# One double-width product for F and an earlier B0 in a two-layer adapter kernel (one Trainium2 core)

## The chip, the cores and the metric

The kernel runs on one core of one Trainium2 chip. The metric is the device time of one execution in microseconds. The core has TensorE (PE in the profile, its weight loads PEld), VectorE (DVE), ScalarE (ACT), GpSimd (POOL) and SyncE (SP); each of them works through its instructions in the order in which they are written, and they wait for one another on semaphores. All transfers are issued from the SP queue.

## The reference

Two linear layers with low-rank adapters, each added to its input, on x of 8 x 256 rows and 1024 columns in float32. Cut to what matters:

```python
# layer 0: 4 x 512 rows; one of 5 adapters per group, rank 32
x = x + x @ W0.T + 0.5 * (x @ A0[label]) @ B0.T
# layer 1: 8 x 256 rows; one of 32 adapters per row group, rank 16
x = x + x @ W1.T + b + 2.0 * (x @ A1[slot]) @ B1[slot]
```

The labels pick the adapters at run time.

## The kernel before

The two layers are folded into one matrix. With D = I + W0 and E = I + W1, the product E D is made first on the chip (the first stage), and then applied to x in two further stages of two 512-row chunks each. Each of the three products is done by a seven-product scheme over 512 x 512 blocks (`ORDER`: A11 B11, A12 B21, S1 T1, ...), in which S1 to S4 and T1 to T4 are sums of blocks made on VectorE.

Each float32 operand is split into a rounded part (h, made on ScalarE, line 233) and the remaining part (l, made on VectorE, line 234), and each product of blocks is done in three passes: h h, h l, l h. A block product has four output tiles of 128 x 512 and four quarters of the inner dimension, so 48 products of 128x128 weights and 512 columns.

Beside the block products stand small ones for the adapters. In the first stage these are: D, the rows B0 times the blocks of W1 (`down`, lines 472 to 479), C, the blocks of W0 times A1 (`across`, lines 481 to 488), and F, B0 times A1 (lines 540 to 543). For F the stationary operand is a 128-column tile of `b0s`, in which the rounded part of B0 stands in columns 0 to 31 and 64 to 127, and the remaining part in columns 32 to 63; the moving operand is A1's rounded part (`a1s[0]`) or remaining part (`a1s[1]`), 128 columns each, 8 quarters of the inner dimension each: 16 products into one bank of PSUM. The rows of the result that belong to the rounded and the remaining part of B0 are then added (`rows_sum`, lines 494 to 497: a copy on ScalarE, an add on VectorE) and put into four row groups (`four_rows`, lines 499 to 504). `fsrc` is used only in the second stage (`load_a0`, `low_f`).

The order of TensorE's work is the order in which `pe(...)` is called. After A11 B11 come `down` (eight products), `across` (twelve), F (sixteen), and then tile 0 of A12 B21. The order on ScalarE, VectorE, GpSimd and SP isn't written out: `Plan.rehearse` goes through all jobs with an assumed duration for each and gives each job a due time, from TensorE's rehearsed time backwards; a lane takes, of the jobs whose inputs are there soonest, the one that is due first. A job whose `due` is set by hand in the code keeps it if it is the earlier one. Loading A1 needs the labels: SP reads eight labels from `label_t` into registers (line 194) and issues eight transfers, one for each slot (line 451).

Of the kernel before, what the change touches and what calls it, by code (L numbers as in the profile page):

```python
# [6 lines left out]
ALU = mybir.AluOpType  # L7
F32 = mybir.dt.float32
F32R = mybir.dt.float32r
# [10 lines left out]
NK = 8  # L20
# [101 lines left out]
def bass_blocks(nc, x, labels, w0, a0, b0, w1, bias, a1, b1, out):  # L122
    ctx = ExitStack()
    with ctx:
        def sb(name, shape, dt, where=None):
            return (where or ctx).enter_context(nc.sbuf_tensor(name, shape, dt))
# [9 lines left out]
        bstk = [sb(f"bstk{n}", [128, 1024], F32R) for n in range(2)]  # L136
        mb = {n: sb("m_" + n, [128, 4, 512], F32) for n in ("11", "12", "21", "22")}
        small = ExitStack()
        a1s = [sb(f"a1{j}", [128, NK, 128], F32R, small) for j in "hl"]
        a1raw = sb("a1raw", [128, 8, NK, 16], F32, small)  # L140
        b0s = sb("b0s", [128, NK, 4, R], F32R, small)
        ct = [sb(f"ct{j}", [128, 512], F32R, small) for j in "hl"]
# [12 lines left out]
        dtmp = [sb(f"dtmp{n}", [R, 512], F32, temps) for n in range(3)]  # L155
# [8 lines left out]
        ps = [ctx.enter_context(nc.psum_tensor(f"ps{i}", [128, 512], F32)) for i in range(8)]  # L164
# [7 lines left out]
        plan = Plan()  # L172

        def tk(*name):
            return tokens.setdefault(name, Token())
# [4 lines left out]
        def act(waits, emit, token, took):  # L180
            plan.put("act", waits, emit, token, took)

        def dve(waits, emit, token, took):
            plan.put("dve", waits, emit, token, took)
# [4 lines left out]
        def transfer(waits, pairs, s, token, kb, numbers=(), top=0, count=1):  # L189

            def emit(eng):
                for i in numbers:
                    if i not in label:
                        label[i] = eng.value_load(label_t[:, i:i + 1], min_val=0, max_val=top)  # L194
                for dst, src in pairs():
                    eng.dma_start(dst, src).then_inc(s, 16)  # L196
            plan.put("sp", list(waits) + ([tk("labels")] if numbers else []), emit, token, 0.45 * count)
            plan.jobs[-1].kb = kb
            counts[s] = counts.get(s, 0) + 16 * count
            token.sem, token.value = s, counts[s]  # L200

        bank_free = {}

        def pe(out_ap, lhs, rhs, start, waits=(), name=None):
            n = 1
            for s in rhs.shape[1:]:
                n *= s
            plan.put("pe", waits, (out_ap, lhs, rhs, start), tk(*name) if name else Token(), max(n / 2400 + 0.0133, 0.107))
            plan.jobs[-1].named = bool(name)
# [11 lines left out]
        act([tk("eye")], lambda e: e.activation(eye_r[:, :], eye[:, :], ACT.Copy), tk("eye_r"), 0.3)  # L221
        dve([], lambda e: e.memset(astk[:, :, :, 64:128].bitcast(F32), 0.0), tk("zero"), 0.9)
        transfer([], lambda: [(label_t[:, :], labels)], s_lab, tk("labels"), 1)
        plan.jobs[-1].due = 7.0
        transfer([], lambda: [(bias_t[:, :], bias)], s_bias, tk("bias"), 4)


# [27 lines left out]
        def split_b(n, ks):  # L255

            stage, name = n // 7, ORDER[n % 7][1]
            src = where[stage, name][:, ks[0]:ks[-1] + 1, :]
            used = [4 * n + k - NB for k in ks]
            spare = [tk("Bk", m // 4, m % 4) for m in used if m >= 0]  # L260
            hi, lo = (br[j][:, slot(n, ks[0]):slot(n, ks[-1]) + 1, :] for j in range(2))
            split([tk("f", stage, name, k) for k in ks], spare, src, hi, lo, same(("B", 0, n), ks), same(("B", 1, n), ks), len(ks))
# [31 lines left out]
        def ybank(stage, i):  # L294
            return 4 - 4 * (stage % 2) + i
# [145 lines left out]
        for k in range(4):  # L441
# [2 lines left out]
            split_a(0, (k,))  # L444
            split_b(0, (k,))
        transfer([], lambda: [(b0raw[:, :, :].rearrange("p k r -> p (k r)"), b0[:, :])], s_b0, tk("b0"), 128)
        act([tk("b0")], lambda e: e.activation(  # L447
            b0s[:, :, :, :], b0raw[:, :, :].unsqueeze(2).to_broadcast([128, NK, 4, R]), ACT.Copy), tk("b0h"), 1.1)
        dve([tk("b0h")], lambda e: e.tensor_tensor(  # L449
# [44 lines left out]
        def rows_sum(bank, done, cols, dst, name, spare):  # L494

            act([done] + spare, lambda e: e.activation(dtmp[0][:, cols], ps[bank][R:2 * R, cols], ACT.Copy), tk("t", *name), 0.6)
            dve([tk("t", *name)], lambda e: e.tensor_tensor(dst, ps[bank][0:R, cols], dtmp[0][:, cols], ALU.add), tk("sum", *name), 0.7)

        def four_rows(src, dst, ready, name):

            for q in (0, 1, 3):
                act([ready], lambda e, q=q: e.activation(dst[q * R:(q + 1) * R, :], src, ACT.Copy, scale=S0), tk("four", q, *name), 0.65)
            dve([tk("four", 0, *name)], lambda e: e.scalar_tensor_tensor(
                out=dst[2 * R:3 * R, :], in0=src, scalar=S0, in1=dst[0:R, :].bitcast(F32), op0=ALU.mult, op1=ALU.subtract), tk("four", 2, *name), 0.7)
# [22 lines left out]
        Y = [ybank(0, i) for i in range(4)]  # L527
# [10 lines left out]
        for k in range(4):  # L538
            split_b(1, (k,))
        for k in range(NK):  # L540
            for j in range(2):
                pe(ps[Y[1]][:, 0:128], b0s[:, k, :, :].rearrange("p q r -> p (q r)"), a1s[j][:, k, :], k == 0 and j == 0,
                   [tk("b0l"), tk("a1", j, k // 4)], ("fd",) if (k, j) == (NK - 1, 1) else None)
        rows_sum(Y[3], tk("dn", 0), slice(0, 512), dtmp[1][:, :], ("e",), [])
        rows_sum(Y[1], tk("fd"), slice(0, 128), dtmp[2][:, 0:128], ("f",), [tk("sum", "e")])
        bank_free[Y[1]] = [tk("sum", "f")]
        four_rows(dtmp[2][:, 0:128], fsrc, tk("sum", "f"), ("f",))
        sum_s1(0)
        sum_t1(0)
# [405 lines left out]
```

How the kernel before makes its waits and increments, by code:

```python
def wait_all(eng, waits, done):  # L115
    for t in waits:
        if done.get(t.sem, 0) < t.value:
            done[t.sem] = t.value
            eng.wait_ge(t.sem, t.value)
# [71 lines left out]
            def emit(eng):  # L191
                for i in numbers:
                    if i not in label:
                        label[i] = eng.value_load(label_t[:, i:i + 1], min_val=0, max_val=top)
                for dst, src in pairs():
                    eng.dma_start(dst, src).then_inc(s, 16)
# [680 lines left out]
        def run(eng, name, s):  # L877
            done = {}
            for job in order[name]:
                wait_all(eng, job.waits, done)
                job.emit(eng).then_inc(s, 1)
# [3 lines left out]
            @block.sync  # L885
            def _(eng):
                done = {}
                for job in order["sp"]:
                    wait_all(eng, job.waits, done)
                    job.emit(eng)
                for s in s_keep.values():
                    eng.wait_ge(s, counts[s])
# [13 lines left out]
            @block.tensor  # L906
            def _(eng):
                done = {}
                wait_all(eng, [tk("fzero")], done)
                zeros = fstk[:, 0, :]
                for i in range(WARM):
                    ins = eng.matmul(ps[7][:, :], zeros, zeros.unsqueeze(1).to_broadcast([128, 4, 128]), start=True, stop=True)
                ins.then_inc(s_pe, 1)
                for job in tensor:
                    wait_all(eng, job.waits, done)
                    out_ap, lhs, rhs, first = job.emit
```

## Time and profile before

| what | value |
|---|---|
| time, median of 3 runs | 295.98 us (293.93, 295.98, 296.96) |
| profiled execution | 294.4 us, its span 292.7 us |
| TensorE (PE) busy | 286.7 us, 98% of the span |
| weight loads (PEld) busy | 239.6 us, 82% |
| VectorE busy | 223.2 us, 76% |
| ScalarE busy | 143.5 us, 49% |
| granted TensorE clock | 1.000 (mean of the core) |

The span runs from the first to the last instruction of one profiled execution, and times in the rows are counted from its start. A row of a timeline has the start, the duration, the engine, the line of the kernel, the operation and its output and inputs, how many like it were merged (x2), and in brackets the idle time of the engine before it and what ended that. Matmuls overlap, so the distance from start to start tells their pace, not the duration. Buffer numbers are left out of names, so `ar0h` is the rounded left operand of products 0, 2, 4 and `ar1h` that of 1, 3, 5.

### The profile page before, as it was taken

What the parts mean: (1) busy time and instruction counts of PE and PEld (TensorE: products, weight loads), DVE (VectorE), ACT (ScalarE), POOL (GpSimd) and SP (SyncE); (2) the same over time, 40 slices, a digit from 0 to 9 for tenths busy, and PEclk for the clock granted to TensorE, in tenths of its full rate; (3) what the DMA queues carried; (4) which work ended last, traced back from release to release, by engine and by line L of the source; (5) the groups of instructions that cost most, each with busy time, mean ns of one, the idle gap of its engine ahead of it and who ended that gap; (6) DMA issues with size and microseconds to landing.
All of it is one profiled execution on the core that took longest, in us unless ns stands there. A gap on an engine that the chain in (4) does not pass through costs nothing.

```text
span 292.7 us, 3668 instructions
## 1 busy us (share of the span) xinstructions
PE 286.7 (98%) x1340; PEld 239.6 (82%) x1340; DVE 223.2 (76%) x265; ACT 143.5 (49%) x194; POOL 5.0 (2%) x13
## 2 busy tenths in 40 slices
PE   8979999999999999999999999999999999999996
PEld 5858888888888888888888888888988888888885
DVE  5557998898988989999985999839295956687400
ACT  5377539452563862827282632637474463505021
POOL 0000300000000000010000000000010000000000
PEclk9999999999999999999999999999999999999999
DMA  7389800220645101116432438240101100012222
GB/s 252 93 301 394 271 2 2 72 73 0 202 114 152 36 2 36 36 24 172 168 113 68 140 106 290 91 129 37 38 0 72 72 2 0 0 72 91 91 99 81
DMA packets 18628, 29.21 MB, mean 100 GB/s; under 512 B 2994, under 2 KB 5426, under 8 KB 18610
## 3 DMA queue, kind: packets, MB, share of 16 engines
q1 hardware_dynamic: 18610, 28.98, 30.2%
q8 instruction: 10, 0.16, 0.2%
q14 instruction: 8, 0.07, 0.1%
HBM read 20.58 MB, written 8.39 MB: 99 GB/s over the span
## 4 chain that ended last, share of the span: by engine, by line
PE 93%; SPq 3%; DMA 2%; issue 1%; ACT 0%; DVE 0%
PE ps L917 93%; SPq L196 2%; SPq L194 1%; DMA label_t<-in_labels 1%; DMA b0raw<-in_b 1%; ACT b0s L447 0%; DVE b0s L449 0%; DVE keep_s L731 0%
## 5 line engine op out<-in xcount | busy, mean ns | idle before, releaser
L917 PE MATMUL ps<-brh,ar0h 128*128 128x512 f32 (+1 forms) x180 | 69.2, 390 | 0.1
L917 PE MATMUL ps<-brl,ar0h 128*128 128x512 f32 (+1 forms) x180 | 68.3, 385 | 0.0
L917 PE MATMUL ps<-brh,ar0l 128*128 128x512 f32 (+1 forms) x180 | 68.2, 384 | 0.0
L233 ACT ACTIVATE brh<-w_B 128x1024 fp32r<-128x1024 f32 (+1 forms) x40 | 38.8, 969 | 57.6 <-PE ps L917 50.6
L917 PE MATMUL ps<-brh,ar1h 128*128 128x512 f32 x160 | 62.5, 391 | 0.0
L917 PE MATMUL ps<-brl,ar1h 128*128 128x512 f32 x160 | 62.3, 390 | 0.0
L917 PE MATMUL ps<-brh,ar1l 128*128 128x512 f32 x160 | 62.3, 389 | 0.0
L234 DVE TENSOR_TENSOR brl<-w_B,brh 128x1024 fp32r<-128x1024 f32 (+1 forms) x40 | 44.5, 1113 | 18.5 <-ACT brh L233 18.3
L917 PEld LDWEIGHTS ps<-brh,ar0h 128*128 128x128 f32 x180 | 34.3, 191 | 7.4 <-ACT ar0h L233 0.8
L917 PEld LDWEIGHTS ps<-brh,ar0l 128*128 128x128 f32 x180 | 33.8, 188 | 6.8
L917 PEld LDWEIGHTS ps<-brl,ar0h 128*128 128x128 f32 x180 | 33.9, 188 | 6.5
L917 PEld LDWEIGHTS ps<-brh,ar1l 128*128 128x128 f32 x160 | 30.0, 188 | 6.4
L917 PEld LDWEIGHTS ps<-brh,ar1h 128*128 128x128 f32 x160 | 30.1, 188 | 6.0
L917 PEld LDWEIGHTS ps<-brl,ar1h 128*128 128x128 f32 x160 | 30.1, 188 | 5.9
L234 DVE TENSOR_TENSOR ar0l<-w_A,ar0h 128x1024 fp32r<-128x1024 f32 (+1 forms) x16 | 17.3, 1086 | 0.8 <-ACT ar0h L233 0.5
L344 DVE SCALAR_TENSOR_TENSOR keep_s<-ps,bias_t,keep_s 128x512 f32<-128x512 f32 x16 | 11.6, 747 | 6.7 <-PE ps L917 6.6
L233 ACT ACTIVATE ar0h<-w_A 128x1024 fp32r<-128x1024 f32 (+1 forms) x16 | 15.0, 945 | 1.6 <-DVE w_A L281 0.8
L234 DVE TENSOR_TENSOR ar1l<-w_A,ar1h 128x1024 fp32r<-128x1024 f32 (+1 forms) x14 | 14.9, 1068 | 0.7 <-ACT ar1h L233 0.5
L386 ACT ACTIVATE keep_s<-ps,bias_t 128x512 f32<-128x512 f32 x7 | 4.8, 687 | 21.3 <-PE ps L917 21.3
L281 DVE TENSOR_TENSOR w_B<-w_B 128x1024 f32<-128x1024 f32 x12 | 14.4, 1220 | 0.2
L233 ACT ACTIVATE ar1h<-w_A 128x1024 fp32r<-128x1024 f32 (+1 forms) x14 | 12.9, 929 | 0.6 <-PE ps L917 0.5
L917 PE MATMUL ps<-pstk,dstk 128*128 128x512 f32 x32 | 12.4, 389 | 0.0
(116 smaller groups left out, 355.7 us busy)
## 6 DMA issues: line engine op xcount, KB each, us to landing
w_B<-in_x SPq DMA_DIRECT2D x32, 256.0 KB, 2.8
out_z<-keep_s SPq DMA_DIRECT2D x23, 256.0 KB, 2.0
w_B<-in_w SPq DMA_DIRECT2D x16, 256.0 KB, 5.1
w_A<-in_w SPq DMA_DIRECT2D x16, 256.0 KB, 4.9
raw<-in_b SPq DMA_DIRECT2D x64, 32.0 KB, 1.7
out_z<-keep_w SPq DMA_DIRECT2D x8, 256.0 KB, 2.1
raw<-in_a SPq DMA_DIRECT2D x8, 128.0 KB, 2.2
a1raw<-in_a SPq DMA_DIRECT2D x8, 64.0 KB, 1.8
```

The lines of the kernel that those rows point to most:

```text
L194: label[i] = eng.value_load(label_t[:, i:i + 1], min_val=0, max_val=top)
L196: eng.dma_start(dst, src).then_inc(s, 16)
L233: act(waits + spare, lambda e: e.activation(hi, src, ACT.Copy, scale=scale), h, 0.2 + 0.43 * wide)
L234: dve([h], lambda e: e.tensor_tensor(lo, src, hi.bitcast(F32), ALU.subtract), l, 0.15 + 0.54 * wide)
L281: lambda e, part=part, ins=ins: e.tensor_tensor(place[:, part, :], ins[0], ins[1], op),
L344: dve(waits + [tk("bias")], lambda e: e.scalar_tensor_tensor(out=dst, in0=z, scalar=bias_t[:, 4 * a + i:4 * a + i + 1], in1=other, op0=ALU ...
L386: act([done, tk("bias"), tk("stored", stage, "s1", i, 0, 0)], lambda e: e.activation(s1, z, ACT.Identity, bias=bias_t[:, 4 + i:5 + i]), to ...
L917: ins = eng.matmul(out_ap, lhs, rhs, start=first, stop=False, skip_group_check=True)
```

## The change

`a1s` becomes two halves of one tile `a1hl` in which, for each quarter of the inner dimension, the 128 columns of the rounded part and the 128 of the remaining part lie side by side. F is computed by one product of 256 columns for each quarter, eight in all; `rows_sum` works on 256 columns, and one more VectorE add puts the two halves of 128 columns together. The transfer of the labels gets a due time of 4.0 in place of 7.0, and that of B0 a due time of 9.0, which it didn't have.

```diff
-        a1s = [sb(f"a1{j}", [128, NK, 128], F32R, small) for j in "hl"]
+        a1hl = sb("a1hl", [128, NK, 2, 128], F32R, small)
+        a1s = [a1hl[:, :, j, :] for j in range(2)]
...
         transfer([], lambda: [(label_t[:, :], labels)], s_lab, tk("labels"), 1)
-        plan.jobs[-1].due = 7.0
+        plan.jobs[-1].due = 4.0
...
         transfer([], lambda: [(b0raw[:, :, :].rearrange("p k r -> p (k r)"), b0[:, :])], s_b0, tk("b0"), 128)
+        plan.jobs[-1].due = 9.0
...
         for k in range(NK):
-            for j in range(2):
-                pe(ps[Y[1]][:, 0:128], b0s[:, k, :, :].rearrange("p q r -> p (q r)"), a1s[j][:, k, :], k == 0 and j == 0,
-                   [tk("b0l"), tk("a1", j, k // 4)], ("fd",) if (k, j) == (NK - 1, 1) else None)
+            pe(ps[Y[1]][:, 0:256], b0s[:, k, :, :].rearrange("p q r -> p (q r)"), a1hl[:, k, :, :].rearrange("p j c -> p (j c)"), k == 0,
+               [tk("b0l"), tk("a1", 0, k // 4), tk("a1", 1, k // 4)], ("fd",) if k == NK - 1 else None)
         rows_sum(Y[3], tk("dn", 0), slice(0, 512), dtmp[1][:, :], ("e",), [])
-        rows_sum(Y[1], tk("fd"), slice(0, 128), dtmp[2][:, 0:128], ("f",), [tk("sum", "e")])
-        bank_free[Y[1]] = [tk("sum", "f")]
+        rows_sum(Y[1], tk("fd"), slice(0, 256), dtmp[2][:, 0:256], ("fhl",), [tk("sum", "e")])
+        bank_free[Y[1]] = [tk("sum", "fhl")]
+        dve([tk("sum", "fhl")], lambda e: e.tensor_tensor(dtmp[2][:, 0:128], dtmp[2][:, 0:128], dtmp[2][:, 128:256], ALU.add), tk("sum", "f"), 0.3)
         four_rows(dtmp[2][:, 0:128], fsrc, tk("sum", "f"), ("f",))
```

The new due times change the order that the rehearsal gives. First the start of the SP queue: `w_A11` and `w_B11` are the four tiles each of the first operands, `label_t` the labels, `b0raw` B0, `w_B21` and `w_A12` the next operands. Before, after the four first transfers:

```order
L196 DMA label_t<-in_labels 1x16
L196 DMA w_B11<-in_w1 128x512
L196 DMA w_A11<-in_w0 128x512
L196 DMA w_B11<-in_w1 128x512
L196 DMA w_A11<-in_w0 128x512
L194 TENSOR_LOAD label_t
...
L196 DMA a1raw<-in_a1 128x128
L196 DMA b0raw<-in_b0 128x256
L196 DMA w_B21<-in_w1 128x512
```

With the change, after the two first transfers:

```order
L197 DMA label_t<-in_labels 1x16
L197 DMA w_B11<-in_w1 128x512
L197 DMA w_A11<-in_w0 128x512
L197 DMA w_B11<-in_w1 128x512
L197 DMA w_A11<-in_w0 128x512
L197 DMA b0raw<-in_b0 128x256
L197 DMA w_B11<-in_w1 128x512
L197 DMA w_A11<-in_w0 128x512
L195 TENSOR_LOAD label_t
...
L197 DMA a1raw<-in_a1 128x128
L197 DMA w_B21<-in_w1 128x512
```

The labels go from fifth to third place, and B0 from behind the eight loads of A1 to eighth place, ahead of the last tile of each first operand.

ScalarE in the opening, from the third tile of the first operands on (`b0s` is B0's rounding, `ar1h` the next tile's left operand, `dtmp0<-ps5` the copy of F's rows, `m_11<-ps` copies of the first product's results). Before:

```order
L233 ACTIVATE ar0h<-w_A11 128x4x128
L233 ACTIVATE brh<-w_B11 128x512
L233 ACTIVATE ar0h<-w_A11 128x4x128
L233 ACTIVATE a1h<-a1raw 128x8x4x16
L447 ACTIVATE b0s<-b0raw 128x1024
L233 ACTIVATE a1h<-a1raw 128x8x4x16
L233 ACTIVATE brh<-w_B21 128x512
...
L233 ACTIVATE brh<-w_B21 128x512
L353 ACTIVATE m_11<-ps2 128x512
L233 ACTIVATE ar1h<-w_A12 128x4x128
L496 ACTIVATE dtmp0<-ps5 32x128
```

With the change:

```order
L234 ACTIVATE ar0h<-w_A11 128x4x128
L449 ACTIVATE b0s<-b0raw 128x1024
L234 ACTIVATE brh<-w_B11 128x512
L234 ACTIVATE ar0h<-w_A11 128x4x128
L234 ACTIVATE a1hl<-a1raw 128x8x4x16 x2
L234 ACTIVATE brh<-w_B21 128x512
...
L234 ACTIVATE brh<-w_B21 128x512
L498 ACTIVATE dtmp0<-ps5 32x256
L234 ACTIVATE ar1h<-w_A12 128x4x128
L354 ACTIVATE m_11<-ps3 128x512
```

B0's rounding now stands ahead of the fourth tiles of the first operands instead of between the two halves of A1, and the copy of F's rows stands ahead of the last rounding of `ar1h` instead of behind it.

ScalarE later in the first stage, in the third product (`dtmp0<-ps7` is the copy of the rows of the second `down`, `ctile` the transposed C). Before:

```order
L233 ACTIVATE brh<-m_12 128x1024
L496 ACTIVATE dtmp0<-ps7 32x512
L233 ACTIVATE ar0h<-w_A21 128x4x256
...
L363 ACTIVATE m_22<-ps4 128x512
L522 ACTIVATE ctile<-ps6 128x512
L502 ACTIVATE dstk<-dtmp2 32x512 x3
```

With the change:

```order
L234 ACTIVATE brh<-m_12 128x1024
L234 ACTIVATE ar0h<-w_A21 128x4x256
...
L364 ACTIVATE m_22<-ps4 128x512
L524 ACTIVATE ctile<-ps6 128x512
L498 ACTIVATE dtmp0<-ps7 32x512
L364 ACTIVATE m_22<-ps5 128x512
L504 ACTIVATE dstk<-dtmp2 32x512
```

The copy from bank 7, which frees that bank for the next `across`, moves behind the copy of the transposed tile.

## Rows read from the trace of the kernel before

**Rows 1.** The page: the span, and the shares by line of the last chain.
```profile
span 292.7 us, 3668 instructions
...
PE ps L917 93%; SPq L196 2%; SPq L194 1%; DMA label_t<-in_labels 1%; DMA b0raw<-in_b 1%; ACT b0s L447 0%; DVE b0s L449 0%; DVE keep_s L731 0%
```

**Rows 2.** Timeline, all engines: TensorE from 16.6 to 19.1.
```profile
16.64 0.39 PE L917 MATMUL ps<-brh,ar0l 128*128 128x512 f32 x1
...
18.71 0.50 PE L917 MATMUL ps<-brh,b0s 128*128 128x512 f32 x1 [1.68 <-DVE b0s L449]
...
19.05 0.40 PE L917 MATMUL ps<-brl,b0s 128*128 128x512 f32 x1
```

**Rows 3.** The last chain in order of time: start, us, what; four of its pieces.
```profile
2.68 2.88 DMA label_t<-in_labels
...
14.36 2.76 DMA b0raw<-in_b
17.14 1.06 ACT b0s L447
18.23 0.44 DVE b0s L449
```

**Rows 4.** Timeline, all engines: the first operands' preparation and use, and A1.
```profile
8.44 0.63 ACT L233 ACTIVATE ar0h<-w_A 128x512 fp32r<-128x512 f32 x1 [0.17 <-DVE w_A L439]
...
10.71 0.69 DVE L234 TENSOR_TENSOR ar0l<-w_A,ar0h 128x512 fp32r<-128x512 f32 x1
...
14.15 0.39 PE L917 MATMUL ps<-brh,ar0h 128*128 128x512 f32 x1
...
14.61 0.39 PE L917 MATMUL ps<-brh,ar0l 128*128 128x512 f32 x1
...
16.43 0.69 DVE L234 TENSOR_TENSOR a1l<-a1raw,a1h 128x512 fp32r<-128x512 f32 x1 [5.03 <-ACT a1h L233]
```

**Rows 5.** Timeline of the SP queue in the opening.
```profile
3.92 0.43 SPq L196 DMA_DIRECT2D w_B<-in_w  x1
4.40 0.43 SPq L196 DMA_DIRECT2D w_A<-in_w  x1
10.35 3.97 SPq L196 DMA_DIRECT2D a1raw<-in_a  x8
14.36 0.43 SPq L196 DMA_DIRECT2D b0raw<-in_b  x1
14.84 0.43 SPq L196 DMA_DIRECT2D w_B<-in_w  x1
```

**Rows 6.** Timeline of TensorE: F's first product, and the product after its last.
```profile
23.38 0.22 PE L917 MATMUL ps<-a1h,b0s 128*128 128x128 f32 x1
...
25.11 0.45 PE L917 MATMUL ps<-brh,ar1h 128*128 128x512 f32 x1
```

**Rows 7.** Timeline of TensorE: first pair of sixteen 256-column products; what follows them.
```profile
118.83 0.40 PE L917 MATMUL ps<-brh,astk 128*128 128x256 f32 x2
...
120.74 0.40 PE L917 MATMUL ps<-brh,ar0h 128*128 128x512 f32 x1
```

**Rows 8.** Timeline of ScalarE: copies of row sums and transposed tile.
```profile
21.31 0.59 ACT L496 ACTIVATE dtmp<-ps 32x512 f32<-32x512 f32 x1
...
25.31 0.27 ACT L496 ACTIVATE dtmp<-ps 32x128 f32<-32x128 f32 x1 [0.22 <-PE ps L917]
...
44.40 0.60 ACT L522 ACTIVATE ctile<-ps 128x512 f32<-128x512 f32 x1 [0.24 <-PE ps L917]
```

**Rows 9.** Timeline of VectorE: preparing the second and fourth products.
```profile
25.12 0.69 DVE L234 TENSOR_TENSOR ar1l<-w_A,ar1h 128x512 fp32r<-128x512 f32 x1
...
49.75 1.23 DVE L234 TENSOR_TENSOR brl<-w_B,brh 128x1024 fp32r<-128x1024 f32 x1 [0.92 <-ACT brh L233]
```

**Rows 10.** Timeline of TensorE: the first use of `ar1l`'s last part.
```profile
27.72 0.39 PE L917 MATMUL ps<-brh,ar1l 128*128 128x512 f32 x1
```

**Rows 11.** Timeline of TensorE: the next `across`, into bank 7.
```profile
47.03 0.39 PE L917 MATMUL ps<-ar0h,a1h 128*128 128x512 f32 x1
```

## The prediction

> **What bounds the kernel now.** I read the page first: a span of 292.7 us, of whose last chain TensorE's product line holds 93% [rows 1]. So time is saved only where TensorE stands still or where it does less. Then I read the timeline around the one place in mid-kernel where it waits: after the product that starts at 16.64 nothing starts until 18.71, and the releaser is VectorE's part of B0 (1.68 us in the profile's own count) [rows 2]. The chain in order of time tells why B0 is late [rows 3]: the SP queue waits for the labels (2.88 us from issue to landing), reads eight of them, issues the eight loads of A1, and only then issues B0, which lands 2.76 us later; ScalarE rounds it (1.06), VectorE takes the rest (0.44). Behind that wait TensorE runs to the end without another.
>
> **The sum, part by part.**
>
> *Term 1, the wait for B0.* From 16.64 to 18.71 are 2.07 us [rows 2]; one product of 512 columns takes 0.23 (14.15 to 14.61 is two of them [rows 4]), so 1.84 is standing still. The first product after it takes 0.34 to the next start (18.71 to 19.05 [rows 2]), 0.11 more than the pitch. Together 1.95, if nothing else is late there.
>
> Where B0 goes: the change gives it the eighth place on the SP queue, which today goes to a tile at 3.92, and the last two tiles of the first operands move to 4.40 and, one pitch of 0.48 on (14.36 to 14.84), 4.88 [rows 5]. With today's 2.76 to landing [rows 3] B0 is there at 6.7, and the 1.06 on ScalarE comes after the rounding that today ends at 9.07 (8.44 + 0.63 [rows 4]): it ends near 10.2, its VectorE part near 10.7. TensorE asks at 16.64 + 0.23 = 16.87, so B0 has six microseconds of cover. Who is queued behind it: the last quarter's roundings on ScalarE and VectorE, and the later landing of their tiles. Today the last of them ends at 11.40 (10.71 + 0.69); with 1.06 and 0.44 more in front, and 0.48 on the queue, at most 13.4 if all three add up. TensorE asks for that quarter's first part at 14.15 and for the remaining part at 14.61 [rows 4]. So the opening costs nothing; without this cover it would cost up to 1.98.
>
> The labels go to third place. That delays the second tiles by their own issue, under 0.5; these have the start of the second quarter to meet, which the first quarter's twelve products cover. The labels move two pitches up, from 2.68 to 1.7, and by the 2.88 of [rows 3] land at 4.6, while the SP queue is at work until 4.88 + 0.43 = 5.3. Today they land at 2.68 + 2.88 = 5.56. The reads of labels start some 0.2 earlier, and so does A1. A1's first remaining part is ready today at 17.12 (16.43 + 0.69 [rows 4]), and the product that asks for it will come eight products after 16.87, at 18.7: 1.6 of cover. I put the gain or loss here at nothing.
>
> *Term 2, the small product F.* Sixteen products of 128 columns run from 23.38 to 25.11 [rows 6]: 1.73 us, 0.108 each. Eight of 256 columns take their place. Such a product stands elsewhere in the trace: from 118.83 to 120.74 there are sixteen, 0.119 each [rows 7]. 8 x 0.119 = 0.96, so 0.77 is saved. Bounds: 0.81 if each costs half a 512-column product (0.115), nothing if each costs as much as two of the old ones; I take 0.77 because [rows 7] are of the same shape and change the weights at every product too. The Trainium skill ("TensorE: Matmul & The Clock Gate", section "Back-to-back issue gap") speaks against this term: in its formula for an isolated product the spacing is the columns at 2.4 GHz plus 2.5 ns, so two of 128 columns cost what one of 256 does, and the estimate from its cycle table is a saving of 0.02 and a sum of 292.4. By the trace a 128-column product here takes twice what that formula gives, so the rule doesn't hold for this stretch.
>
> *What is added behind F.* The partial sums are now 256 wide: ScalarE's copy of F lies between today's 0.27 for 128 columns and 0.59 for 512 [rows 8], VectorE's add likewise, and one VectorE add of 32x128 is new. F's result is needed only in the second stage, so only what is queued behind counts, and there is something: ScalarE's copy of F now stands ahead of the last rounding of the next tile's left operand. F ends at 23.38 - 1.95 + 0.96 + 0.28 = 22.7 (0.28 is what a pair of [rows 7] takes beyond one pitch, 0.40 - 0.12); the copy ends by 23.3, the rounding (0.63) by 23.9, VectorE's remaining part (0.69) by 24.6. Today that part is ready at 25.81 (25.12 + 0.69 [rows 9]) and is asked for at 27.72 [rows 10], which becomes 27.72 - 2.72 = 25.0. The cover is 0.4. The loads of that tile are issued 0.48 (B0 gone from their front) plus 0.2 earlier. If nothing of that preparation moved forward, TensorE would wait 25.81 - 25.0 = 0.81. So the cost is between 0 and 0.81; I take 0, since the works that stood before it (B0's 1.06 and 0.44) are gone from this stretch.
>
> *What is only moved.* ScalarE's copy of the next row sum now stands behind the copy of the transposed tile, 44.40 + 0.60 today [rows 8], so 42.3 after the shift; with 0.59 for itself and about 0.67 on VectorE the bank is free at 43.6. TensorE wants the bank at 47.03 [rows 11], shifted 44.3: 0.7 of cover. VectorE may meanwhile stand waiting for some 1 us (the copy's 0.59 and what is left of the transposed tile's), with the preparation of the fourth product behind it; today VectorE is idle 0.92 before that preparation [rows 9], which about pays for it. Nothing, then, and at most 1.0. Output and input transfers in the second stage change places on the queue; no product has waited there, and I put them at nothing too.
>
> Sum: 1.95 + 0.77 = 2.72. The profiled execution took 294.4 (span 292.7), so it would take **291.7**. The runs shown are 293.93, 295.98 and 296.96; the mean of these and the profiled one is 295.3, the median 0.5% above the profiled one. I state the time against that mean: 295.3 - 2.7 = 292.6.
>
> **The rivals.**
>
> *The wait passes on to the next tile, or to the bank of the row sum.* For it: covers of only 0.4 and 0.7 once TensorE is 2.7 ahead. Against it: the preparing engines lose the same work that made B0 late. Price 0.81 to 1.0: the profiled execution at 292.5 to 292.7, a gain of 0.6%.
>
> *The merge brings nothing.* If the columns alone set the pitch of F, eight products of 256 columns cost what the sixteen of 128 do, term 2 is nothing, and the time is 294.4 - 1.95 = 292.45. Against it: 0.108 for 128 columns and 0.119 for 256 in the same trace [rows 6, 7]. This is the case that the formula quoted above from the Trainium skill would make.
>
> *It gains more than the sum.* Two landings of small transfers, 2.88 and 2.76, stand on the chain today [rows 3]; an execution in which they take longer is later by as much. After the change the labels have 0.7 of cover, A1 1.6 and B0 six. If the runs at 295.98 and 296.96 were late for that reason, they come down to about 291.7, which is 1.4% to 1.8%. For it: the spread is as large as such a landing. Against it: nothing shows that the spread arises there.
>
> *Slower.* B0's rounding now stands in fixed order ahead of the last quarter's roundings, so a late B0 holds up the first product itself. It decides from a landing of B0 at about 10.3 on (9.07 plus the spare 1.2 that 13.4 leaves to 14.61); the loss of all 2.72 needs a landing near 13.0, nine microseconds after issue, and then the time is 294.4 and more beyond. The 2.76 of [rows 3] speaks against it.
>
> **How the numbers follow.** Forecast 0.62, the wait that passes on 0.14, no gain from the merge 0.05, more than the sum 0.14, slower 0.05 (with what I have overlooked). A measurement of this kernel tells about 1% from no change, here 2.95 us. The forecast of 2.72 is 0.92%, just short of it; with runs that differ by 1% I give it 0.45 to come out over the bound. Faster: 0.62 x 0.45 + 0.14 + 0.01 = 0.43. Slower by over 1%: 0.04. Same: 0.53. Range: the lowest run less the upper bounds, 293.93 - 1.95 - 0.81 - 0.2 = 291.0, a little under it for a run as low again, 290.8; above, the median less the smaller gain of the first rival, 295.98 - 1.91 = 294.1, and 0.6 for the run that is higher still: 294.7.
>
> **What will show it.** TensorE's product after the one at 16.6 starts at 16.9, with no wait for B0; the eight products of F span about 0.96; the first product of the next tile starts near 22.4; ScalarE's B0 rounding runs near 9.1 in the opening; everything behind is 2.7 earlier, up to the last store. Wrong it would be if the table of waits showed TensorE waiting for a remaining part of the second left operand near 25, for the row sum near 44, or for the last quarter near 14; or if F's eight products took 1.7.

## The result

| executions | before | changed |
|---|---|---|
| median of 6 each | 295.25 us (293.93 to 296.96) | 292.28 us (291.67 to 292.81) |
| ratio, 95% interval | | 0.9894 (0.9859 to 0.9929) |
| profiled execution | 294.4 us, span 292.7 | 292.81 us, span 291.1 |

The changed kernel takes 292.28 us; 292.6 was forecast. A second comparison gave 292.52 against 295.83, a ratio of 0.9884 (0.9835 to 0.9932). The forecast held the time, but not for its reasons alone: two things that it didn't count, one on either side, nearly cancel. That the total came out so near is luck.

The first shows in the list of executions with their mean granted clock. Of 67 more executions of the kernel before, on five chips, 39 ran at a mean clock of 0.998 to 1.000 and took 294.40 us on average (293.76 to 295.2); 24 ran at 0.994 and took 296.34 (295.66 to 297.96); four at 0.987 to 0.989 took 298.0 to 298.6 (the ratios leave out the two longest of these, 298.5 and 298.62, as slow ones). All twelve executions of the changed kernel ran at 0.998 to 1.000 and took 292.34 on average. So at an equal clock the change is worth 294.40 - 292.34 = 2.06 us, less than the 2.72 of the sum, and the rest of its gain is that the executions with a lower clock are gone.

**The profile after.** First the page: span and shares of the last chain [rows 1]. TensorE's product line has 90%; a transfer of `w_A` and ScalarE's `ar1h` are new on it, the transfers of B0 and of the labels are gone.

```profile
span 291.1 us, 3655 instructions
...
PE 286.1 (98%) x1332; PEld 238.0 (82%) x1332; DVE 223.9 (77%) x266; ACT 144.2 (50%) x194; POOL 4.0 (1%) x13
...
PE ps L919 90%; SPq L197 3%; DMA w_A<-in_w 2%; SPq L195 1%; ACT ar1h L234 0%; ACT brh L234 0%; ACT dtmp L498 0%; ACT m L354 0%; DVE keep_s L733 0%
```

TensorE's timeline in the places of [rows 2] and [rows 6], and on into the first tile of the second product:

```profile
16.27 0.39 PE L919 MATMUL ps<-brh,ar0l 128*128 128x512 f32 x1
16.49 0.39 PE L919 MATMUL ps<-brh,b0s 128*128 128x512 f32 x1
16.72 0.39 PE L919 MATMUL ps<-brl,b0s 128*128 128x512 f32 x1
...
21.03 1.12 PE L919 MATMUL ps<-a1hl,b0s 128*128 128x256 f32 x8
21.98 0.40 PE L919 MATMUL ps<-brh,ar1h 128*128 128x512 f32 x1
...
23.59 0.39 PE L919 MATMUL ps<-brl,ar1h 128*128 128x512 f32 x1
23.90 0.50 PE L919 MATMUL ps<-brh,ar1l 128*128 128x512 f32 x1
25.09 0.50 PE L919 MATMUL ps<-brh,ar1h 128*128 128x512 f32 x1 [0.69 <-ACT ar1h L234]
```

The product that asked for B0 at 18.71 now starts at 16.49, one pitch (0.22) behind its neighbour. F spans 21.98 - 21.03 = 0.95 us instead of 1.73. Then a new wait: from 23.90 to 25.09 are 1.19 us for one product, 0.96 more than the pitch, and the releaser is the last rounding of `ar1h`. Why it was late stands in ScalarE's timeline:

```profile
19.35 0.59 ACT L354 ACTIVATE m<-ps 128x512 f32<-128x512 f32 x1
20.68 0.63 ACT L234 ACTIVATE ar1h<-w_A 128x512 fp32r<-128x512 f32 x1 [0.75 <-DMA w_A<-in_w]
...
23.00 0.60 ACT L354 ACTIVATE m<-ps 128x512 f32<-128x512 f32 x1
23.49 0.62 ACT L234 ACTIVATE brh<-w_B 128x512 fp32r<-128x512 f32 x1
24.14 0.38 ACT L498 ACTIVATE dtmp<-ps 32x256 f32<-32x256 f32 x1
24.42 0.61 ACT L234 ACTIVATE ar1h<-w_A 128x512 fp32r<-128x512 f32 x1
```

ScalarE stood 0.75 for the second tile of `w_A` (issued at 15.57, there at 20.66), and F's copy (24.14) now stands ahead of the last rounding. In the kernel before, the last two roundings were these:

```profile
22.94 0.62 ACT L233 ACTIVATE ar1h<-w_A 128x512 fp32r<-128x512 f32 x1
...
24.46 0.63 ACT L233 ACTIVATE ar1h<-w_A 128x512 fp32r<-128x512 f32 x1
```

The last one moved from 24.46 to 24.42, that is, hardly at all, while TensorE starts on this tile 3.13 us earlier (21.98 against 25.11).

The order in the opening is as forecast: SP issues the labels at 1.74 and B0 at 3.92, ScalarE rounds B0 from 9.64, and VectorE's last part of the first operands starts at 12.05, where 10.71 stood [rows 4].

```profile
1.74 0.33 SPq L197 DMA_DIRECT2D label_t<-in_labels  x1
...
3.92 0.43 SPq L197 DMA_DIRECT2D b0raw<-in_b  x1
...
9.64 1.04 ACT L449 ACTIVATE b0s<-b0raw 128x1024 fp32r<-128x1024 f32 x1
...
12.05 0.69 DVE L235 TENSOR_TENSOR ar0l<-w_A,ar0h 128x512 fp32r<-128x512 f32 x1
```

### The profile page after: what moved, and what is told of

The parts are those of the page before. It is cut to its first block, busy times and chain, and to the rows that moved or that the text cites. A ratio compares the mean times of both kernels' runs of the same rounds, so it can differ in the third digit from the quotient of the medians.

```text
span 291.1 us, 3655 instructions
## 1 busy us (share of the span) xinstructions
PE 286.1 (98%) x1332; PEld 238.0 (82%) x1332; DVE 223.9 (77%) x266; ACT 144.2 (50%) x194; POOL 4.0 (1%) x13
## 4 chain that ended last, share of the span: by engine, by line
PE 90%; SPq 4%; DMA 2%; ACT 1%; issue 1%; DVE 0%
PE ps L919 90%; SPq L197 3%; DMA w_A<-in_w 2%; SPq L195 1%; ACT ar1h L234 0%; ACT brh L234 0%; ACT dtmp L498 0%; ACT m L354 0%; DVE keep_s L733 0%
## 5 line engine op out<-in xcount | busy, mean ns | idle before, releaser
L919 PEld LDWEIGHTS ps<-brh,ar0h 128*128 128x128 f32 x180 | 33.7, 188 | 7.7 <-ACT ar0h L234 1.3
```

The source lines that it names most:

```text
L919: ins = eng.matmul(out_ap, lhs, rhs, start=first, stop=False, skip_group_check=True)
```

## The experiments

Two questions: which part of the change brings what, and why some four in ten executions of the kernel before take 2 us more than the others. At first I held the late landing of the labels for the cause; the run with B0 alone turned the question to the clock. "Full clock" means executions whose mean granted clock was 0.998 or more; their mean time stands beside the 294.40 of the kernel before. On the four chips that have such executions of the kernel before their mean lies between 294.24 and 294.54, so runs on different chips can't be told apart to better than some 0.3 us.

**The changed kernel once more.** No edit.

> The changed kernel once more, for a second trace. Theory (two terms, of which a part is given back): B0's wait (1.95 us) and 0.77 at F are gone in every execution, and what is given back is a wait of TensorE for the rounded or remaining part of the second left operand near 24 to 26 us, because a tile of it lands late; it varies from execution to execution between 0 and 1.3 us. So the span lies between 290.0 (no such wait) and 291.3, and this trace shows B0's wait gone and a wait near 25 of another size than the 0.7 of the table of waits after. Rival (the wait near 25 is set by the order on ScalarE, not by a landing): the same wait of 0.7 to 1.2 again, with ScalarE busy without a pause from 17 on. Ratio 0.989 +- 0.004 by both.

Measured: 292.52 (291.85 to 292.81), ratio 0.9884 (0.9835 to 0.9932). The profiled execution took 291.85, span 290.1, and its table of waits has no wait but that ahead of the first product:

```profile
PE ps L914 <- DVE fstk L217: 1.3, 1, 1.3
```

So the wait for `ar1h` is not in every execution. A smaller loss is: from the first product of the second operands' first two tiles to the next `down` are 24 products, 5.44 us at 0.2267. The stretch took 25.11 to 30.66 = 5.55 before, 21.98 to 28.88 = 6.90 in the first trace of the changed kernel, and 21.96 to 27.93 = 5.97 in this one, here without a counted wait, in four starts that are 0.07 to 0.15 late each:

```profile
23.81 0.39 PE L919 MATMUL ps<-brh,ar1l 128*128 128x512 f32 x1
24.11 0.50 PE L919 MATMUL ps<-brh,ar1h 128*128 128x512 f32 x1
24.45 0.39 PE L919 MATMUL ps<-brl,ar1h 128*128 128x512 f32 x1
24.83 0.50 PE L919 MATMUL ps<-brh,ar1l 128*128 128x512 f32 x1
25.17 0.40 PE L919 MATMUL ps<-brh,ar1h 128*128 128x512 f32 x1
```

**The merge alone.** The labels and B0 stay where they were.

```diff
-            for j in range(2):
-                pe(ps[Y[1]][:, 0:128], ..., a1s[j][:, k, :], ...)
+            pe(ps[Y[1]][:, 0:256], ..., a1hl[:, k, :, :].rearrange("p j c -> p (j c)"), ...)
```

> F by eight products of 256 columns, labels and B0 loaded where the kernel before loads them. By the sum: 0.77 us less (0.81 with the pitch after the last product), B0's wait of 1.7 stays in the table of waits, no wait near 25, since TensorE gets there only 0.8 earlier: ratio 0.9973, 294.5 against 295.25. Rival (columns alone set the pitch of F, the merge brings nothing): 1.000. Rival (the order around F costs something of its own): above 1.000.

Measured: 295.57, ratio 0.9998 (0.9965 to 1.0032): nothing, in the medians. But nine of its twelve executions ran at 0.992 to 0.994 (295.06 to 297.05). The three at full clock took 293.58, which is 0.82 less than before at full clock, and the wait for B0 (1.7 us) is still in the trace. By these three the merge pays its 0.77; in the medians the executions with a lower clock hide it, nine of twelve here and twelve of the 23 of the kernel before beside them.

**The early loads alone.** F stays as it was.

```diff
         transfer([], lambda: [(label_t[:, :], labels)], s_lab, tk("labels"), 1)
-        plan.jobs[-1].due = 7.0
+        plan.jobs[-1].due = 4.0
...
         transfer([], lambda: [(b0raw[:, :, :].rearrange("p k r -> p (k r)"), b0[:, :])], s_b0, tk("b0"), 128)
+        plan.jobs[-1].due = 9.0
```

> Labels third and B0 eighth on the SP queue, F by sixteen products of 128 columns as before. By the sum: 1.95 us less, and little or no wait near 25, since TensorE comes there 0.8 later than in the full change: ratio 0.9934, 293.3 against 295.25. If more than the sum was gained because executions of the kernel before are late by the landings of labels and B0: ratio 0.990 or lower, and the runs spread over 1 us instead of 3.

Measured: 292.38 (291.79 to 292.83), ratio 0.9875 (0.9825 to 0.9924), as much as the whole change; all six at full clock, 292.32, 2.08 less than before. Parts against whole at full clock: 2.08 + 0.82 = 2.90, the whole 2.06, so 0.84 is given back when both are done (the 0.82 rests on three executions). A part of the loss is in this trace already: the 24 products behind F take 28.84 - 22.91 = 5.93 us, 0.38 more than before, though F's copy stands behind the last rounding of `ar1h` here (24.98 and 24.32).

```profile
22.91 0.45 PE L918 MATMUL ps<-brh,ar1h 128*128 128x512 f32 x1
...
28.84 0.39 PE L918 MATMUL ps<-brh,b0s 128*128 128x512 f32 x1
```

**The labels alone.**

```diff
         transfer([], lambda: [(label_t[:, :], labels)], s_lab, tk("labels"), 1)
-        plan.jobs[-1].due = 7.0
+        plan.jobs[-1].due = 4.0
```

> Only the labels move up, from fifth to third place; B0 stays behind A1, F as before. By the sum: the SP queue is free at 4.83 instead of waiting until 5.56 for the labels, so A1 and B0 come 0.7 earlier and B0's wait shrinks from 1.8 to 1.1: ratio 0.9976. If late label landings make the slower executions of the kernel before: the spread of the runs shrinks from 3 us to about 2 and the ratio is 0.995. If B0's own landing makes them: the spread stays.

Measured: 293.4 (293.1 to 294.15), ratio 0.9935 (0.9908 to 0.9961). The wait for B0 is 0.8 in the trace, and all twelve executions are at full clock: 293.49, 0.91 less than before. The spread, 4.5 us for the kernel before in this comparison, is 1.05.

**B0 alone.**

```diff
         transfer([], lambda: [(b0raw[:, :, :].rearrange("p k r -> p (k r)"), b0[:, :])], s_b0, tk("b0"), 128)
+        plan.jobs[-1].due = 9.0
```

> B0 alone goes ahead of the first operands' last tiles; the labels stay in fifth place and F keeps its sixteen products. The forecast's sum: term 1 alone, 1.95 us off, so 293.9 against a median before of 295.83, and a spread of some 4 us as before. If it is the late landing of the labels that makes the slower executions of the kernel before, then it does so through B0, which is issued behind the reads of the labels; here only A1 hangs on them, which has 1.6 us of cover, so the slower executions come down as well: 292.4 to 292.8 in the median (as with labels and B0 both early), a spread under 2 us. If the labels being fifth hurts by A1 too: 293.4 and more, with TensorE waiting for a remaining part of A1 in F or in the twelve products before it.

Measured: 292.68 (292.33 to 294.43, eight executions, seven of them up to 293.01), ratio 0.9938 (0.9914 to 0.9962), all at full clock. The profiled execution is the one at 294.43, and its chain shows a late landing of the labels, 4.83 us after issue instead of 2.88 [rows 3]:

```profile
2.68 4.83 DMA label_t<-in_labels
...
17.26 4.16 DMA w_B<-in_w
...
26.36 0.53 ACT ar1h L233
26.93 3.28 PE ps L918 x12
```

So labels that land late exist: this execution took 1.8 us more than the mean of the other seven, though only A1 and the tiles behind it hang on the labels here, and its chain goes by way of `ar1h` and not of A1. The median lies where the expectation put it for late labels. But the clock stayed at 1.000 in that execution. That separates two things which I had taken for one: late labels, which scatter single executions, and a clock of 0.994, which so far came only with the wait for B0. Without that wait (this run, the early loads, the changed kernel) none was below 0.998.

**The kernel before once more.** No edit, one execution.

> The kernel before once more, for a second trace. If the slower executions (296 and more) come from the labels: in a slower one the labels land 2 us or more later than the 2.88 us from issue of the first trace, B0's loads and TensorE's wait for B0 are later by the same amount, and all else is as in the first trace. In a faster one (294.3) the trace is as the first. If the slower ones come from elsewhere, the wait for B0 stays at about 1.8 us in a slower execution too.

Measured: 293.62, a wait of 1.6 and labels that land after 2.76 us. It was an execution at full clock and so tells nothing of the others.

**The wait filled.** Eight products that nobody uses are put between the first product and `down`, so that TensorE works where it waited.

```diff
+        for r in range(8):
+            pe(ps[Y[1]][:, :], ar[0][0][:, r % 4, 3, :], b_tile(0, 3, 0), True)
+            plan.jobs[-1].took = 0.0
         down(Y[3], 0, 0, True, ("dn", 0))
```

> The kernel before with eight products of 512 columns that nobody uses, put on TensorE between the first product and the products that wait for B0 (1.81 us of work in a wait of 1.84). Theory of the clock: in the slower executions of the kernel before (296 to 297, mean granted clock 0.994) TensorE's clock fell after the wait for B0; with the wait filled it stays at 1.000 in every execution, the slower ones vanish, and the median is that of the faster ones, 294.3, in spite of the added work. Theory of the labels: the slower executions are late because the labels land late and B0 with them; filling the wait changes nothing of that, the time scatters from 294 to 297 as before, some with a clock under 1.000 or not.

Measured: 294.65 (293.95 to 295.75), ratio 0.9994 (0.9973 to 1.0016); all twelve at 1.000, while of the 20 executions of the kernel before beside them eight ran at 0.994 (295.7 to 296.76) and twelve at full clock (294.54 on average). The trace has the added products where the wait was, and B0's first product at the same 18.71 as before:

```profile
16.75 1.97 PE L920 MATMUL ps<-brh,ar0h 128*128 128x512 f32 x8
18.71 0.50 PE L920 MATMUL ps<-brh,b0s 128*128 128x512 f32 x1
```

The clock theory holds in its main point: where TensorE doesn't stand still there, no execution is at 0.994. The median came down by less than I expected (294.65, not 294.3), and the times stand in two groups at the same clock: seven executions at 293.95 to 294.67, five at 295.13 to 295.75. So about one microsecond of the slower executions can come without the clock. Labels that land late could do that; no trace of one of the five was taken.

**The wait made longer.** ScalarE goes over B0 once more, into a tile that is free then, ahead of the rounding that counts.

```diff
-        act([tk("b0")], lambda e: e.activation(
-            b0s[:, :, :, :], ..., ACT.Copy), tk("b0h"), 1.1)
+        act([tk("b0")], lambda e: [e.activation(
+            t, ..., ACT.Copy) for t in (ctile[...], b0s[:, :, :, :])][1], tk("b0h"), 1.1)
```

> The kernel before with one more pass of ScalarE over B0 (into a tile that is free then) ahead of B0's rounding: 1.06 us more in front of TensorE's wait, nothing else in another place. Theory of the clock: a wait of 2.9 us lets the clock fall in nearly every execution; the mean granted clock is about 0.994 and the time 294.3 + 1.06 + 1.8 = 297.2, with 1.8 from a clock that is 0.6% short over 294 us; the trace shows TensorE at 1.2 GHz somewhere behind the wait. Theory of the labels alone: 294.3 + 1.06 = 295.4 in the faster executions at a clock of 1.000, and up to 299 in the slower ones; a scatter as before.

Measured: 296.96 (294.88 to 298.7), ratio 1.008 (1.0045 to 1.0114). Seven of nine executions had a fallen clock: three at 0.994 (296.64 to 296.96), four at 0.988 or 0.989 (298.34 to 298.7); two ran at 1.000 (294.88, 295.61). The profiled one is the 294.88, with 2.63 us of standing still and no fall.

```profile
19.20 0.50 PE L917 MATMUL ps<-brh,b0s 128*128 128x512 f32 x1 [2.63 <-DVE b0s L449]
```

So at this length the clock falls in most executions but not in all, and what decides between them no row shows.

**Longer still.** Two passes more; one execution, for a trace of the fallen clock.

```diff
-        act([tk("b0")], lambda e: e.activation(
-            b0s[:, :, :, :], ..., ACT.Copy), tk("b0h"), 1.1)
+        act([tk("b0")], lambda e: [e.activation(
+            t, ..., ACT.Copy) for t in (ctile[...], dstk[...], b0s[:, :, :, :])][2], tk("b0h"), 1.1)
```

> Two more passes of ScalarE over B0 ahead of its rounding, so that TensorE waits some 3.8 us: a trace of the clock, which the profiles so far have not shown below full speed. Theory of the clock: a stretch behind the wait at 1.2 GHz (granted clock 0.5), in which 512-column products follow at 0.45 us instead of 0.227; a stretch of 3.5 us if the mean clock is 0.994, of 7 us if it is 0.988 (0.6% of 294 us are 1.76 us, lost at half speed in 3.5). Time 294.4 + 2.1 + 1.8 to 3.5 = 298.3 to 300.0. Theory that only the wait counts: 296.5, clock 1.000 throughout.

Measured: 298.41 at a mean clock of 0.988. The page's clock line shows it, in tenths, in the third and fourth slice of 40:

```profile
PEclk9977999999999999999999999999999999999999
```

By stretches (start and end, the stretch's length, busy time of TensorE, its weight loads, VectorE, ScalarE and GpSimd with the number of instructions, then the granted clock, DMA share, GB/s):

```profile
18.00:18.50 0.50, 0.00 (x0) 0.00 (x0) 0.00 (x0) 0.50 (x1) 0.00 (x0) 1.00 1.00 389
18.50:19.00 0.50, 0.00 (x0) 0.00 (x0) 0.00 (x0) 0.50 (x2) 0.00 (x0) 0.57 1.08 414
19.00:20.00 1.00, 0.00 (x0) 0.00 (x0) 0.08 (x1) 1.00 (x2) 0.00 (x0) 0.50 1.05 318
20.00:21.00 1.00, 0.60 (x2) 0.51 (x3) 0.91 (x2) 1.00 (x3) 0.00 (x0) 0.50 1.04 402
21.00:24.00 3.00, 3.00 (x9) 2.32 (x8) 3.00 (x6) 1.97 (x4) 0.00 (x0) 0.50 1.04 391
24.00:25.00 1.00, 1.00 (x4) 0.81 (x3) 0.30 (x2) 0.78 (x2) 0.00 (x0) 0.50 1.03 395
25.00:25.50 0.50, 0.50 (x3) 0.40 (x2) 0.50 (x2) 0.48 (x2) 0.00 (x0) 0.60 1.07 397
25.50:26.00 0.50, 0.50 (x3) 0.39 (x3) 0.50 (x2) 0.50 (x2) 0.00 (x0) 1.00 1.07 393
```

and in TensorE's timeline:

```profile
16.11 0.39 PE L917 MATMUL ps<-brh,ar0l 128*128 128x512 f32 x1
20.40 0.80 PE L917 MATMUL ps<-brh,b0s 128*128 128x512 f32 x1 [3.90 <-DVE b0s L449]
20.99 0.63 PE L917 MATMUL ps<-brl,b0s 128*128 128x512 f32 x1
...
24.83 0.63 PE L917 MATMUL ps<-ar0h,a1l 128*128 128x512 f32 x1
25.26 0.46 PE L917 MATMUL ps<-ar0h,a1h 128*128 128x512 f32 x1
25.56 0.39 PE L917 MATMUL ps<-ar0l,a1h 128*128 128x512 f32 x1
```

TensorE's last product ended at 16.50 (16.11 + 0.39). Its clock went from 2.4 to 1.2 GHz between 18.5 and 19, while it stood still, and back to 2.4 between 25 and 25.5, after five microseconds of products without a pause. The ten products from 20.99 to 25.26 are 0.427 apart instead of 0.227: ten times 0.2 is 2.0 us, and the product ahead of them, at 20.40, is 0.25 longer to the next start than in [rows 2] (0.59 against 0.34). B0's first product starts 1.69 later than there (20.40 against 18.71: the stop is 2.22 longer, 3.90 against 1.68, and the opening was 0.53 faster). Together that is 3.94, and the execution is 298.41 - 294.40 = 4.0 above before's mean at full clock. That mean is from other chips; the one execution of the kernel before beside this one took 297.96, at 0.994. The Trainium skill ("TensorE: Matmul & The Clock Gate", section "Wait — 56ns, not 53.3ns?") gives 426.7 ns for 512 columns at the lower clock, and the row agrees.

**The next tile's loads and roundings earlier, with the change.** The first tile of A12 and of B21 are loaded ahead of A1, and ScalarE's copies of the first product and of F are made to wait for the roundings of `ar1h` and `brh`. For that the calls that split the second right operand (`split_b(1, ...)`) move ahead of the first product's last tiles.

```diff
-                spare = {0: [], 1: ...
+                spare = {0: [tk(m, 0, 1, min(3, i + 2)) for m in "AB"], 1: ...
...
             load_w("A12", k)
+            if k < 1:
+                plan.jobs[-1].due = 10.9
             load_w("B21", k)
+            if k < 1:
+                plan.jobs[-1].due = 10.9
...
+        for k in range(4):
+            split_b(1, (k,))
         for i in range(4):
             step(0, i, 3, ("P", 0, i))
...
-        for k in range(4):
-            split_b(1, (k,))
...
-        rows_sum(Y[1], tk("fd"), slice(0, 256), dtmp[2][:, 0:256], ("fhl",), [tk("sum", "e")])
+        rows_sum(Y[1], tk("fd"), slice(0, 256), dtmp[2][:, 0:256], ("fhl",), [tk("sum", "e"), tk("A", 0, 1, 3), tk("B", 0, 1, 3)])
```

> The whole change, and with it the first tile of each operand of the second product is loaded ahead of A1, and ScalarE's copies of the first product's results and of F stand behind the roundings of those operands. If the merge's 0.77 us is given back in many executions by the wait for the second left operand near 25 us, this wait is gone and the full sum of 2.72 us (profiled 291.7 against 294.4) comes in nearly every execution: median 291.7 to 291.9 against 292.4 of the whole change, spread under 0.8 us. If what gives it back lies elsewhere (the row sum near 44 us, the pitch of what follows), the median stays at 292.3 to 292.5. If the two early tiles make A1 late, TensorE waits for A1's remaining part near 18 and the time is 292.5 to 293.5.

Measured: 291.27 (290.94 to 292.74), ratio 0.99 (0.9869 to 0.9931) against 294.35 beside it; mean of the six 291.50, which is 2.90 less than before at full clock, the sum of the two parts done apart, and 2.74 less than the ten executions at full clock beside it (294.24). The 24 products behind F take 27.24 - 21.57 = 5.67 us:

```profile
20.62 1.11 PE L923 MATMUL ps<-a1hl,b0s 128*128 128x256 f32 x8
21.57 0.40 PE L923 MATMUL ps<-brh,ar1h 128*128 128x512 f32 x1
...
27.24 0.39 PE L923 MATMUL ps<-brh,b0s 128*128 128x512 f32 x1
```

**The same without the merge.** F again as sixteen products of 128 columns.

> As the run before it (labels, B0 and the first pair of tiles early, ScalarE's copies behind the roundings), but F as sixteen products of 128 columns. If the merge is worth its 0.77 us wherever nothing waits behind it: 0.6 to 0.8 us slower than the run before it, 292.4 to 292.6. If the merge is worth nothing at all: the same time as the run before it, within 0.2 us.

Measured: 292.1 (291.93 to 292.99), ratio 0.9923 (0.9895 to 0.9951); 0.83 slower than the run before it in the medians, 0.73 in the means (292.23 against 291.50). Where nothing waits behind it, the merge is worth what the trace said. F's products here:

```profile
20.66 0.22 PE L922 MATMUL ps<-a1h,b0s 128*128 128x128 f32 x1
...
22.40 0.45 PE L922 MATMUL ps<-brh,ar1h 128*128 128x512 f32 x1
```

1.74 us against the 0.95 above.

**The early pair of tiles alone, with the change.** As two above, without the waits for ScalarE's copies.

> The whole change with the first tile of each operand of the second product loaded ahead of A1, but ScalarE's copies left where the change puts them. If the late tiles are what gives the merge's 0.77 us back near 25 us, the early load alone is enough: 291.1 to 291.6 in the median, as with both (291.27), TensorE without a wait before 26 us in the trace. If the copies of the first product's results and of F in front of the roundings give it back, it stays near the change's own 292.3 to 292.5 and TensorE waits for a tile of the second left operand (ar1h or ar1l). The mean granted clock stays at 0.998 or more in every execution, since TensorE has no long wait in either case.

Measured: 291.93 (291.58 to 293.52), ratio 0.9884 (0.9831 to 0.9937), between the two expectations. The trace has no wait near 25, and the 24 products take 5.46 us (22.56 to 28.02), so in this execution ScalarE's copies didn't have to be told to wait. But the run doesn't part the landing from ScalarE's order, as the expectation wanted: with the early tiles the rehearsal puts F's copy behind the last rounding of `ar1h` by itself.

```profile
22.56 0.62 ACT L234 ACTIVATE ar1h<-w_A 128x512 fp32r<-128x512 f32 x1
23.21 0.38 ACT L502 ACTIVATE dtmp<-ps 32x256 f32<-32x256 f32 x1
```

Between the two profiled executions (291.99 here, 290.94 with the waits) 0.94 is from the opening: B0's first product starts at 17.03 here and at 16.09 there. The opening scatters by such amounts between traces (one pitch behind its last start, the first product ends at 16.18 in the second trace of the kernel before and at 16.87 in the first). What ScalarE's order has done and what the early tiles stays open.

## Why the prediction came out, step by step

*Term 1, the wait for B0: 1.95.* Right at full clock: the early loads alone brought 2.08, the labels alone 0.91 for a wait that went from 1.7 to 0.8. But a wait of TensorE had a second price that the sum left out, because the profiled execution didn't show it. In 28 of the 67 executions of the kernel before the clock fell; 24 of them were longer by 1.95 us on average (296.34 - 294.40), four by 3.9; over all 67 that is 0.9 us. Not all of it need be the clock's. A mean clock of 0.994 over 294.6 us is a loss of about 1.8 at the most (an estimate from these two numbers), less where the low stretch lies in the stop itself, as it does in part in the trace above; and with the wait filled five of twelve executions were one microsecond longer at a clock of 1.000. How the 1.95 divides into lost clock and a longer stop isn't shown. I had taken the mean of the executions as the basis and the profiled one for the sum, and let the difference pass as scatter.

| TensorE stands still before `down` | kernels | executions below 0.998 |
|---|---|---|
| not at all | changed, early loads, B0 alone, filled, the three with the early pair | 0 of 56 |
| 0.8 us | labels alone | 0 of 12 |
| 1.6 to 1.7 us | before, merge alone | 37 of 79 |
| 2.6 us | one pass more | 7 of 9 |
| 3.9 us | two passes more | 1 of 1 |

The lengths are those of one or two traces each, by the profile's own count, and all but the last are from executions at full clock: how long TensorE stood still in an execution of the kernel before whose clock fell, no trace shows. Twenty of the 56 ran on a chip on which the kernel before fell in 2 of 12 only; the strongest rows are the filled wait (0 of 12 beside 8 of 20) and the labels alone (0 of 12 beside 12 of 23). What the Trainium skill says ("TensorE: Matmul & The Clock Gate", section "HAM oscillation — how this bites in real kernels"), that a wait for a transfer makes the next stretch of products start at the lower clock, agrees with the trace of the longest stop (0.427 from start to start behind 3.90 us, there a wait for ScalarE's passes). In the executions of the kernel before only the mean clock points to it, in some and not in others.

*Term 2, the product F: 0.77.* Right in size: 0.95 us instead of 1.73 in the trace, 0.82 alone and 0.73 to 0.83 with the next tile early. The formula of the Trainium skill that the prediction quotes (0.02; "TensorE: Matmul & The Clock Gate", section "Back-to-back issue gap") is one for an isolated product, and the same section says that it counts too little for short products which each load their weights. The trace agrees in that: 128 columns cost 0.108 here, 256 cost 0.119.

*What is added behind F: nothing, cover 0.4.* This step failed. I argued that the work that left the stretch (B0's rounding) would let the second left operand's preparation move forward. It did not, or not enough: the last rounding starts at 24.42 in the first trace and at 23.44 in the second, against 24.46 before, while TensorE comes 3.1 us earlier. In the first trace the chain goes from the landing of its second tile, issued behind A1 (15.57 to 20.66), through ScalarE's other copies and roundings, F's copy the last of them (24.14), to the last rounding; in the second ScalarE waited for no tile of `w_A`. The bound of 0.81 that I put aside is about what it cost: 0.84 by the parts, 0.5 to 1.5 us in the 24 products of the two traces. With the pair of tiles early and the copies behind the roundings it is gone (2.74 to 2.90 less than before), and the merge then pays its 0.73 to 0.83; which of the two does it isn't separated. That is the rival of a wait that passes on, in the place near 25 that it named; the sign of being wrong that the prediction gave came true in the first trace, with `ar1h` in place of the remaining part.

*The opening, the labels, A1.* Nothing was lost there: B0's first product starts at its neighbour's pitch, no wait for A1 appears. One size was wrong without harm: B0 took 4.9 us from issue to landing in the trace, not 2.76, and the six microseconds of cover took that in.

*What is only moved.* The row sum near 44 is no wait either; VectorE stood 1.19 for it, as foreseen, without holding TensorE.

*It gains more than the sum.* The effect was there (the executions at 296 to 297 came down), the reason given was not the whole. Late labels exist (4.83 us once), but the two groups of the kernel before differ in the clock: with the wait filled and the labels where they were the group at 0.994 is gone, and two groups one microsecond apart stay. Whether a late landing is what makes the wait long enough for the clock to fall was not seen; no trace of the kernel before at 0.994 exists.

The forecast subtracted 2.72 from 295.3. The changed kernel does 2.06 at full clock, and 0.9 by the executions with a lower clock that are gone: 2.96, which is 292.34 from the 295.3 of all. That is two errors of opposite sign, 0.66 and 0.9, and luck that they meet.

## What to carry to other kernels

Look at the granted clock of every execution, not only of the profiled one: executions in two groups 0.6% apart with clocks of 1.000 and 0.994 pointed here to a wait of TensorE whose removal was worth more than its length. When TensorE is made to arrive earlier at a place, the thing to check there is when the transfers behind the operands land, since these need not move with it. A part that measures as nothing (the merge alone, 0.9998) can be worth 0.8 us at equal clock; add parts up there.

## What the runs showed of the hardware

In the one trace with a fall TensorE's clock went from 2.4 to 1.2 GHz between 18.5 and 19.0, with the engine's last product ended at 16.50, and back to 2.4 between 25.0 and 25.5, after about five microseconds of products without a pause. The kernels with a stop of 1.6 to 1.7 us in their traces at full clock had a mean clock of 0.987 to 0.994 in 37 of 79 executions; how long the stop was in those 37 isn't known. A stop of 2.63 us passed without a fall in one trace. With eight added products of 512 columns in the stop of 1.7 us the mean clock was 1.000 in twelve of twelve executions, and the ratio to the kernel before was 0.9994 (0.9973 to 1.0016); against its executions at full clock alone the mean was 0.3 us longer (294.85 against 294.54). A transfer of 16 labels from fifth place in the queue landed 2.76 to 3.06 us after issue in five traces whose chain shows it, and 4.83 in a sixth; in a seventh, that of the filled wait, the first read of the labels starts at 6.1, some 3.4 after their issue at 2.68.
